# Two row-sum reciprocals in one VectorE instruction, in the first attention of a two-layer transformer kernel

## The chip, the core and the metric

The kernel runs on one core of one Trainium2 chip. The metric is the device time of one execution, in microseconds (us). An engine is TensorE (PE, with its weight loads shown as PEld), VectorE (DVE), ScalarE (ACT), GpSimd (POOL) or SyncE (SP, which here only issues DMAs). Each engine runs its own instructions strictly in the order in which they were written, and engines wait for each other on semaphores.

## The reference

Eight sequences of 1024 tokens with 256 features pass through two layers: attention, a block-quantised feed-forward, a second attention, and a mixture of low-rank experts. What the change touches is the first attention, cut to what matters:

```python
# x: (8, 1024, 256); 8 heads of 64; V = 32
q = (x @ Mq).reshape(B, H, C, K)          # a plain reshape: heads are mixed with rows
k = (x @ Mk).reshape(B, H, C, K)
v = (x @ Mv).reshape(B, H, C, V)
scores = jnp.einsum('bhqk,bhck->bhqc', q, k).reshape(B * H, C, C)
att = jax.nn.softmax(scores / jnp.sqrt(jnp.float32(K)), axis=1)   # over the queries
out = jnp.einsum('bqhc,bhcd->bqhd', att.reshape(B, C, H, C), v)
```

The softmax normalises over the queries, so each key has a maximum and a sum of its own. The kernel puts 128 keys on the partitions and all 1024 queries along the free dimension; the reciprocal of a key's sum can then be multiplied into that key's row of `v`, which is 32 wide, in place of its 1024 attention weights.

## The kernel before

The eight sequences (b = 0 to 7) are worked through in a software pipeline. One period holds, among others, the feed-forward and second attention of earlier sequences and, in its second part, the first attention of the next sequence (`attn0`) beside that sequence's remaining projections, the query/key preparation of the second attention and the expert layer of the one before. Every engine has its own lanes of generators; each `yield` gives a place in time, and `weave` merges the lanes of one engine by these places when the program is built. Nothing is reordered when it runs.

`attn0` has 64 steps for each sequence, one step for each block of 128 keys and one head. I write a step as (m), with m from 0 to 63; g = m // 8 and c = m % 8. A step goes through six stages on four engines:

- **S(m)**, PE, L459 into `pS`: 16 matmuls (four of 32 columns for each of two operand pairs and two halves) give 128 keys x 1024 queries. `pS` holds two steps, so S(m) waits for exponential (m-2), by semaphore `e0_in`.
- **R(m)**, DVE, L1239: the negated maximum of each row.
- **X(m)**, ACT, L914: the exponential, into one of four buffers `EA[m % 4]`, with the row sum accumulated into column c of `zz`, a tile of eight columns.
- **Z(m)**, DVE, L1256: the reciprocal of that column, into column c of `rz`. It stands at place m+1.45, behind R(m+1).
- **V(m)**, POOL, L1726: the slice of `v` times that reciprocal, into one of four buffers `vs[m % 4]`. It waits for `rz_in` to reach m+1.
- **P(m)**, PE, L560: eight matmuls (each seen as two records) of `vs` by `EA`, accumulated in `pV` over the eight steps of a group. It waits for `vs_in`. Its place is m+3.8, behind S(m+3) and ahead of S(m+4); for c = 0 it is m+4.1, behind S(m+4).

Between these, each engine's queue holds other lanes' work: on PE mostly projections (L459 into `pR`), on DVE the low halves of split operands (L1119), LayerNorm statistics (L1136, L1138), normalisations (L1142, L1272), sums of squares (L1545) and additions (L1133, L1233); on POOL a normalisation of the queries and keys of the second attention (L1814 to L1855). What L1855 writes goes to memory and back by SP's DMAs, and becomes the keys and queries of the second attention. A second attention and a feed-forward follow, whose input `xT` comes by a DMA transpose.

In `ffn_in` (L1272) and other lanes the numbers of steps that count on `pv0_in` or `o0_in` stay as they are. The three lanes of `attn0` on PE, ACT and POOL and the wait of V(m) on `rz_in` are not part of the diff.

Of the kernel before, what the change touches and what calls it, by code (L numbers as in the profile page):

```python
# [54 lines left out]
def build(nc, a, out):  # L55
    with ExitStack() as ctx:

        def sb(name, shape, dt=F32):
            return ctx.enter_context(nc.sbuf_tensor(name, shape, dt))

        def sem(name):
            return ctx.enter_context(nc.semaphore(name))
# [116 lines left out]
        zz = sb("zz", [128, 8])  # L179
        rz = sb("rz", [128, 8])  # L180
# [23 lines left out]
        s0_in, max0_in, e0_in, rz_in, vs_in, pv0_in = (sem(n) for n in ("s0", "max0", "e0", "rz", "vs", "pv0"))  # L204
# [42 lines left out]
        def bank(u):  # L247
            return pR[:, 512 * u.bank:512 * u.bank + 512]
# [858 lines left out]
        def _(e):  # L1107
            reg = e.alloc_register("flag_dve")

            def full(key):  # L1110
                u = ring[key]
                e.wait_ge(r_full[u.bank], u.n)
                return u
# [116 lines left out]
            def attn0(b):  # L1230
                def outputs(g):
                    u = full(("o0T", b, g))
                    e.tensor_tensor(x[b % 2][:, g, :], x[b % 2][:, g, :], bank(u)[:, 0:256], ALU.add).then_inc(r_free[u.bank], 1)  # L1233

                for n in range(69):
                    yield n
                    if n < 64:
                        e.wait_ge(s0_in, 64 * b + n + 1)
                        e.tensor_reduce(nmaxa[:, n % 32:n % 32 + 1], pS[:, 1024 * (n % 2):1024 * (n % 2) + 1024], AXX, ALU.max,  # L1239
                                        negate=True).then_inc(max0_in, 1)  # L1240
                    if n > 4 and (n - 5) % 8 == 7:
                        yield n + .35
                        outputs((n - 5) // 8)
                    if n > 3 and (n - 4) % 8 == 7:
                        yield n + .15
                        g = (n - 4) // 8
                        e.wait_ge(pv0_in, 64 * b + 8 * g + 8)
                        if g:
                            full(("o0T", b, g - 1))
                        e.tensor_copy(oTa[:, :], pV[:, 0:256]).then_inc(o0_in, 1)  # L1250
                    yield n + .45
                    if 0 < n < 65:
                        m = n - 1
                        c = m % 8
                        e.wait_ge(e0_in, 64 * b + m + 1)
                        e.reciprocal(rz[:, c:c + 1], zz[:, c:c + 1]).then_inc(rz_in, 1)  # L1256

            def ffn_in(b):
                xb = x[b % 2]
# [424 lines left out]
            def lanes_y(i):  # L1684
                return [*([first(i + 1, attn0), first(i + 1, projections)] if within(i + 1) else []),
                        *([placed(-6, prep()), placed(-6, prep_low()), prep_heads()] if i < 0 else []),
                        *([v for lane in (moe_x3, moe_gate, moe_M) for v in second(i - 1, lane)] if within(i - 1) else []),
                        *([heads(i), heads_bias(i), heads_norm(i)] if within(i) and i + 1 < NB else
                          [heads_end(), heads_bias(i), heads_norm_end(), heads_by_end(), heads_low_end()] if i + 1 == NB else [])]
# [562 lines left out]
```

## Time and profile before

| | us |
|---|---|
| median of 3 runs | 2958.23 |
| lowest and highest of these | 2956.24, 2965.4 |
| span of the profiled execution | 2954.7 |
| PE busy, share of the span | 2580.8, 87% |
| DVE busy | 2104.1, 71% |
| ACT busy | 1979.9, 67% |
| POOL busy | 1193.4, 40% |
| first attention of sequence 3, S(0) to the end of P(63) | 1031.08 to 1203.63 |

The span is the time between the first and last instruction in the profile, and the median of the unprofiled runs lies 3.5 us above it. The page's busy shares are means over all stages. The part to read is the second part of each period, in which `attn0` runs, and there the waits of one engine for another: views of the waits, the timeline of one engine, and the chain of work that ended last (followed back from the end, at each step to what released it).

### The profile page before, as it was taken

Reading aid. Unit: us, or ns where it says so; the run is one execution under the profiler, and the core shown is the slowest. Engines: PE = TensorE matmul, PEld = TensorE weight load, DVE = VectorE, ACT = ScalarE, POOL = GpSimd, SP = SyncE. Lnnn points to the kernel's source line nnn. Section 1 sums busy time; section 2 is a strip of 40 time slices with the busy share of each in tenths; the row PEclk is TensorE's granted clock in tenths of the full one; section 3 lists DMA queues with packets and bytes.
Section 4 is the critical chain, followed back from the end, with each engine's and each line's share of the span. In section 5 each row is a group of like instructions: output and inputs, shape, how many; then the busy total and the mean of one; then the engine's idle time right before and its main releaser. Section 6 shows DMA issues by size and latency. Waiting matters only on the chain.

```text
span 2954.7 us, 115301 instructions
## 1 busy us (share of the span) xinstructions
PE 2580.8 (87%) x50178; PEld 1403.9 (48%) x50178; DVE 2104.1 (71%) x4266; ACT 1979.9 (67%) x3763; POOL 1193.4 (40%) x1677
## 2 busy tenths in 40 slices
PE   4766786998989989999889989899889999899697
PEld 3434554445644466444554456444654446444233
DVE  6778766866778488875879578775788667775433
ACT  3541255876668866787668866787668776687684
POOL 3563156215642167223653156322662256411210
PEclk9997999999999999999999999999999999999798
DMA  4212332234424252323424253243423253222310
GB/s 127 44 38 46 67 84 69 50 49 86 97 64 81 47 111 62 77 51 73 109 63 75 34 108 79 58 78 58 103 70 66 49 86 84 63 67 47 87 31 16
DMA packets 470460, 203.52 MB, mean 69 GB/s; under 512 B 283289, under 2 KB 459937, under 8 KB 469929
## 3 DMA queue, kind: packets, MB, share of 16 engines
q1 hardware_dynamic: 467960, 194.07, 31.9%
q8 instruction: 413, 6.77, 0.9%
q10 hardware_dynamic: 1968, 1.72, 0.2%
q14 instruction: 119, 0.97, 0.1%
HBM read 46.48 MB, written 32.51 MB: 27 GB/s over the span
## 4 chain that ended last, share of the span: by engine, by line
PE 42%; DVE 29%; ACT 8%; SPq 7%; issue 7%; DMA 5%; POOL 2%; DVEq 0%; ACTq 0%; POOLq 0%
PE pR L459 18%; PE pV L690 9%; DVE nmaxa L1239 8%; PE pS L459 5%; PE pS L650 5%; ACT ub L953 5%; PE pV L560 3%; SPq L1958 2%; PE pR L469 2%; SPq L2155 2%; SPq L2141 1%; DMA xT<-ua 1%; DMA xT<-xhb 1%; DVE ua L1142 1%; DVE ua L1119 1%
## 5 line engine op out<-in xcount | busy, mean ns | idle before, releaser
L953 ACT ACTIVATE ub<-pS 128x512 f32<-128x512 f32 x2048 | 1048.2, 612 | 227.6 <-PE pS L650 227.0
L1239 DVE TENSOR_REDUCE nmaxa<-pS 128x1 f32<-128x1024 f32 x512 | 621.1, 1214 | 249.9 <-PE pS L459 247.2
L914 ACT ACTIVATE ua<-pS,nmaxa 128x1024 f32<-128x1024 f32 x384 | 427.9, 1114 | 406.1 <-DVE nmaxa L1239 403.9
L459 PE MATMUL pS<-ua 128*32 128x512 f16 x8192 | 544.1, 387 | 102.2 <-ACT ua L914 77.4
L690 PE MATMUL pV<-ub,vaug 128*17 128x512 f32 x4096 | 536.7, 597 | 14.6 <-DVE ub L1397 13.2
L1726 POOL TENSOR_TENSOR ua<-ua,rz 128x256 f32<-128x256 f32 x512 | 332.0, 650 | 429.4 <-DVE rz L1256 414.4
L650 PE MATMUL pS<-ub 50*128 50x512 f16 x1920 | 352.0, 386 | 27.6 <-DMA ub<-scr 11.6
L459 PEld LDWEIGHTS pS<-ua 128*32 128x32 f16 x8192 | 210.1, 98 | 273.9 <-ACT ua L914 110.4
L459 PE MATMUL pR<-wgu,xT 128*32 128x352 f16 x6144 | 284.9, 321 | 49.5 <-DMA xT<-ua 24.6
L650 PEld LDWEIGHTS pS<-ub 50*128 50x128 f16 x1920 | 96.5, 93 | 404.4 <-ACT ub L953 334.6
L560 PE MATMUL pV<-ua 128*32 128x128 f32 x6144 | 244.7, 279 | 22.6 <-DVE oTa L1250 12.2
L459 PEld LDWEIGHTS pR<-wgu,xT 128*32 128x32 f16 x6144 | 160.9, 99 | 188.1 <-issue 114.6
L914 ACT ACTIVATE EA<-pS,nmaxa 128x1024 f32<-128x1024 f32 x128 | 142.6, 1114 | 137.1 <-DVE nmaxa L1239 135.9
L560 PEld LDWEIGHTS pV<-ua 128*32 128x32 f32 x6144 | 169.3, 112 | 92.3 <-DVE oTa L1250 25.8
L459 PE MATMUL pR<-wqkv,xT 128*32 128x512 f16 (+1 forms) x3072 | 147.4, 330 | 13.8 <-DMA xT<-xhb 10.2
L1790 POOL CAST xhb<-at_ 128x256 f16<-128x256 f32 x56 | 24.1, 431 | 301.9 <-DVE at_ L1389 253.4
L1771 POOL TENSOR_TENSOR EA<-ua,EA 128x704 f16<-128x704 f32 x28 | 45.5, 1627 | 239.4 <-DVE EA L1348 239.4
L690 PEld LDWEIGHTS pV<-ub,vaug 128*17 128x17 f32 x4096 | 84.7, 96 | 114.4 <-issue 73.9
L459 PE MATMUL pR<-wd,ua 128*32 128x256 f16 x4032 | 130.5, 273 | 3.3 <-DVE ua L1307 1.9
L459 PEld LDWEIGHTS pR<-wd,ua 128*32 128x32 f16 x4032 | 103.9, 97 | 56.5 <-issue 47.9
L459 PE MATMUL pR<-xT,mq 128*32 128x256 f16 x3072 | 98.4, 279 | 26.2 <-DMA xT<-ua 25.2
L1297 DVE SCALAR_TENSOR_TENSOR ua<-ua,pR 128x352 f32<-128x352 f32 x112 | 57.5, 513 | 89.4 <-ACT ua L924 89.4
(262 smaller groups left out, 4062.6 us busy)
## 6 DMA issues: line engine op xcount, KB each, us to landing
ua<-ua SPq DMA_DIRECT2D x384, 128.0 KB, 2.7
ub<-scr SPq DMA_DIRECT2D x264, 64.0 KB, 2.9
scr<-ub SPq DMA_DIRECT2D x30, 512.0 KB, 3.8
x<-in_L_attn_x SPq DMA_DIRECT2D x8, 1024.0 KB, 6.2
between<-x SPq DMA_DIRECT2D x7, 1024.0 KB, 5.0
ub<-between SPq DMA_DIRECT2D x7, 1024.0 KB, 5.9
out<-ub SPq DMA_DIRECT2D x7, 1024.0 KB, 5.4
ub<-scr SPq DMA_DIRECT2D x192, 32.0 KB, 1.8
```

What stands on the lines that cost most here:

```text
L459: i = e.matmul(dst[j:j + 32], w[:, j:j + 32], m, start=start, stop=stop)
L469: return e.matmul(dst, src, ident[0:n, 0:n], is_transpose=True)
L560: i = e.matmul(pV[32 * jl:32 * jl + 32, 128 * jg:128 * jg + 128], vs[n % 4][:, j, :], EA[n % 4][:, 128 * j:128 * j + 128], start=(c == 0 a ...
L650: e.matmul(pS[:, 512 * hl:512 * hl + 512], kk_[row:row + 50, o, 128 * c:128 * c + 128], q[row:row + 50, o, 512 * qh:512 * qh + 512]).then_ ...
L690: i = e.matmul(pV[32 * hl:32 * hl + 17, :], vaug[:, c, 4 * hg + hl, :], EB[(4 * n + hl) % 8], start=(c == 0), stop=(c == 7))
L914: e.activation(EA[n % 4], pS[:, 1024 * (n % 2):1024 * (n % 2) + 1024], ACT.Exp, bias=nmaxa[:, n % 32:n % 32 + 1], accum_out=zz[:, n % 8:n ...
L953: e.activation(EB[(4 * n + hl) % 8], pS[:, 512 * hl:512 * hl + 512], ACT.Exp).then_inc(e1_in, 1)
L1239: e.tensor_reduce(nmaxa[:, n % 32:n % 32 + 1], pS[:, 1024 * (n % 2):1024 * (n % 2) + 1024], AXX, ALU.max, negate=True).then_inc(max0_in, 1)
L1297: e.scalar_tensor_tensor(ht[hv][:, FH:2 * FH], ht[hv][:, 0:FH], 1.0, bank(g)[:, 0:FH], ALU.add, ALU.mult).then_inc(r_free[g.bank], 1)
L1726: e.tensor_tensor(vs[m % 4], vv[:, :, 32 * c:32 * c + 32], rz[:, c:c + 1].unsqueeze(2).to_broadcast([128, 8, 32]), ALU.mult).then_inc(vs_i ...
L1958: e.dma_start(dst[r0:r0 + 64, par::2, o:o + 256], sh[64 * par:64 * par + 64, w, l, :, :]).then_inc(fill0[pair % 2], 16)
L2155: e.dma_start(dst[at:at + 16, o:o + 2, :], scr[b % 2, w_, l, 64 * hg:64 * hg + 64, :].rearrange("(h p d) n -> p d h n", p=2, d=16)[par]).t ...
```

## The change

In DVE's lane of `attn0`, even steps no longer have a reciprocal. At odd steps one instruction takes the reciprocals of two neighbouring columns, c-1 and c, and raises `rz_in` by two. The wait for `e0_in` at the odd step stands as before. The places in the order are unchanged, and so is every other lane.

```diff
                     if 0 < n < 65:
                         m = n - 1
                         c = m % 8
-                        e.wait_ge(e0_in, 64 * b + m + 1)
-                        e.reciprocal(rz[:, c:c + 1], zz[:, c:c + 1]).then_inc(rz_in, 1)
+                        if m % 2:
+                            e.wait_ge(e0_in, 64 * b + m + 1)
+                            e.reciprocal(rz[:, c - 1:c + 1], zz[:, c - 1:c + 1]).then_inc(rz_in, 2)
```

The order of DVE in the first attention of sequence 3, from R(44) to Z(47), before. Names are tiles, output first; `amx`, `small` and `ub` belong to other lanes, and the semaphores waited for stand in brackets:

```order
L1239 TENSOR_REDUCE nmaxa<-pS 128x1 [waits s0]
L1545 TENSOR_REDUCE small<-ub 128x64 [waits sq]
L1233 TENSOR_TENSOR x<-x,pR 128x256 [waits r_full0]
L1256 RECIPROCAL rz<-zz 128x1 [waits e0]
L1239 TENSOR_REDUCE nmaxa<-pS 128x1 [waits s0]
L1256 RECIPROCAL rz<-zz 128x1 [waits e0]
L1239 TENSOR_REDUCE nmaxa<-pS 128x1 [waits s0]
L1133 SCALAR_TENSOR_TENSOR ub<-pR,ub 128x256 [waits r_full1,xb2]
L1272 TENSOR_SCALAR ua<-x,agF,rstdF 128x256 [waits rstdF,fill0_1]
L1272 TENSOR_SCALAR ua<-x,agF,rstdF 128x256 x3
L1256 RECIPROCAL rz<-zz 128x1 [waits e0]
L1239 TENSOR_REDUCE nmaxa<-pS 128x1 [waits s0]
```

The same place in the changed kernel, whose later lines are numbered one higher:

```order
L1239 TENSOR_REDUCE nmaxa<-pS 128x1 [waits s0]
L1546 TENSOR_REDUCE small<-ub 128x64 [waits sq]
L1233 TENSOR_TENSOR x<-x,pR 128x256 [waits r_full0]
L1257 RECIPROCAL rz<-zz 128x2 [waits e0]
L1239 TENSOR_REDUCE nmaxa<-pS 128x1 [waits s0] x2
L1133 SCALAR_TENSOR_TENSOR ub<-pR,ub 128x256 [waits r_full1,xb2]
L1273 TENSOR_SCALAR ua<-x,agF,rstdF 128x256 [waits rstdF,fill0_1]
L1273 TENSOR_SCALAR ua<-x,agF,rstdF 128x256 x3
L1257 RECIPROCAL rz<-zz 128x2 [waits e0]
```

The reciprocal of step 44 between R(45) and R(46) is gone; step 44 is now served by the instruction behind the four L1272. The reciprocal ahead of R(45) serves steps 42 and 43. PE's order is the same in both kernels; its part of the same place, from P(42) to P(44), is this:

```order
L560 MATMUL pV<-ua 32x128 [waits vs]
L560 MATMUL pV<-ua 32x128 x7
L459 MATMUL pR<-wmoe,xT1 32x256 [waits r_free1]
L459 MATMUL pR<-wmoe,xT1 32x256 x23
L459 MATMUL pR<-bt,ub 32x256 [waits r_free2]
L459 MATMUL pR<-bt,ub 32x256 x11
L459 MATMUL pS<-ua 32x512 [waits e0]
L459 MATMUL pS<-ua 32x512 x15
L560 MATMUL pV<-EA3,ua 32x128 [waits vs]
L560 MATMUL pV<-EA3,ua 32x128 x7
L459 MATMUL pS<-ua 32x512 [waits e0]
L459 MATMUL pS<-ua 32x512 x15
```

Nothing has moved here: behind each P(m) stands the work that waits with it.

## Rows read from the trace of the kernel before

**Rows 1.** The page: busy us of each engine, share of the span, instructions.
```profile
PE 2580.8 (87%) x50178; PEld 1403.9 (48%) x50178; DVE 2104.1 (71%) x4266; ACT 1979.9 (67%) x3763; POOL 1193.4 (40%) x1677
```

**Rows 2.** Busy time by engine in sequence 3's first attention: window, length, PE, PEld, DVE, ACT, POOL.
```profile
1031.00:1204.00 173.00, 153.03 (x3818) 103.08 (x3822) 140.16 (x290) 109.09 (x195) 111.87 (x175) 0.99 0.40 91
```

**Rows 3.** The reciprocals, grouped by form: busy us, mean ns, idle before, releaser.
```profile
L1256 DVE RECIPROCAL rz<-zz 128x1 f32<-128x1 f32 x512 | 77.0, 150 | 10.4 <-ACT EA L914 9.6
```

**Rows 4.** Waits between 1031 and 1204 us: total us, times, longest.
```profile
POOL ua L1726 <- DVE rz L1256: 49.9, 31, 13.8
...
DVE nmaxa L1239 <- PE pS L459: 30.3, 21, 10.8
...
PEld pV L560 <- POOL ua L1726: 3.6, 8, 0.9
```

**Rows 5.** Timeline of DVE (start, length in us): Z(42), Z(43), Z(44), R(46), Z(45), L1153, Z(47).
```profile
1152.55 0.15 DVE L1256 RECIPROCAL rz<-zz 128x1 f32<-128x1 f32 x1
...
1156.06 0.15 DVE L1256 RECIPROCAL rz<-zz 128x1 f32<-128x1 f32 x1
...
1157.25 0.15 DVE L1256 RECIPROCAL rz<-zz 128x1 f32<-128x1 f32 x1
1157.32 1.21 DVE L1239 TENSOR_REDUCE nmaxa<-pS 128x1 f32<-128x1024 f32 x1
...
1160.52 0.15 DVE L1256 RECIPROCAL rz<-zz 128x1 f32<-128x1 f32 x1
...
1162.91 1.20 DVE L1153 TENSOR_REDUCE amx<-ua 128x64 f32<-128x1024 f32 x1
1164.03 0.15 DVE L1256 RECIPROCAL rz<-zz 128x1 f32<-128x1 f32 x1
```

**Rows 6.** Timeline of POOL: V(42) and V(50).
```profile
1152.85 0.61 POOL L1726 TENSOR_TENSOR ua<-ua,rz 128x256 f32<-128x256 f32 x1 [2.21 <-DVE rz L1256]
...
1173.03 0.61 POOL L1726 TENSOR_TENSOR ua<-ua,rz 128x256 f32<-128x256 f32 x1
```

**Rows 7.** Timeline of PE: P(42), S(46), S(47), P(44), P(46), P(50).
```profile
1154.53 0.62 PE L560 MATMUL pV<-ua 128*32 128x128 f32 x16
...
1155.98 1.05 PE L459 MATMUL pS<-ua 128*32 128x512 f16 x16
...
1158.63 1.05 PE L459 MATMUL pS<-ua 128*32 128x512 f16 x16 [0.96 <-ACT ua L914]
1159.81 0.64 PE L560 MATMUL pV<-ua 128*32 128x128 f32 x16
...
1163.96 0.61 PE L560 MATMUL pV<-ua 128*32 128x128 f32 x16
...
1173.69 0.65 PE L560 MATMUL pV<-ua 128*32 128x128 f32 x16 [0.44 <-POOL ua L1726]
```

**Rows 8.** The chain that ended last, 1170 to 1198 us, in order of time.
```profile
1171.13 1.95 POOL ub L1855
...
1192.68 4.37 DMA xT<-ua
```

**Rows 9.** Timeline at step 2 of sequence 3: P(2), S(6), Z(3), S(7).
```profile
1044.20 0.61 PE L560 MATMUL pV<-ua 128*32 128x128 f32 x16
...
1045.21 1.05 PE L459 MATMUL pS<-ua 128*32 128x512 f16 x16 [0.40 <-ACT ua L914]
...
1045.57 0.13 DVE L1256 RECIPROCAL rz<-zz 128x1 f32<-128x1 f32 x1
...
1048.71 1.05 PE L459 MATMUL pS<-ua 128*32 128x512 f16 x16 [0.49 <-ACT ua L914]
```

**Rows 10.** Timeline in sequence 1: P(6), the projection behind it, Z(7).
```profile
350.12 0.61 PE L560 MATMUL pV<-ua 128*32 128x128 f32 x16
...
353.21 1.60 PE L459 MATMUL pR<-wgu,xT 128*32 128x352 f16 x24 [2.48 <-DVE ua L1119]
...
353.50 0.15 DVE L1256 RECIPROCAL rz<-zz 128x1 f32<-128x1 f32 x1
```

## The prediction

> **What bounds the kernel now.** I read the page first [rows 1]. PE is busy for 87% of the span and DVE for 71%, so neither is at its limit over the whole. The change only touches the first attention, which runs in about 172 us of each period of some 338 us, so I went to that stretch for sequence 3 [rows 2]. There PE is busy for 153 of 173 us and DVE for 140, while ACT and POOL have 60 us or more to spare. It is a stage of two nearly full engines in fixed order, each waiting now and then for the other.
>
> The waits of the stretch come next [rows 4]. POOL waits for reciprocals for 49.9 us, which is harmless where POOL has nothing late behind it. PE waits for POOL's product V(m) for only 3.6 us (its weight loads, 8 times). DVE waits 30.3 us for scores. The reader should see that V(m) is waited for little because it is early, on average over the even steps about 2.7 us before PE wants it, and that this margin is what the change spends.
>
> **What is removed.** Of 512 reciprocals 256 go [rows 3]. One shows 150 ns, but the next DVE instruction starts 0.07 us behind its start (1157.25 and 1157.32) [rows 5]. So DVE gets back between 256 x 0.07 = 18 us and 256 x 0.15 = 38 us over the whole kernel. I take 0.07, because that is the pitch in the queue. Widening the rest from 128x1 to 128x2 I put at nothing; the 128x256 product on POOL shows no trace of a form that small, and the bound is the whole 0.07 us on the 256 that stay, which would cancel the gain. The gain counts only where DVE sets the pace. In sequence 3 the chain of work that ended last, read step by step up to step 50, passes through about ten of the reciprocals that go, so I count 10 x 0.07 = 0.7 us there, or at most all 32 x 0.07 = 2.2 us.
>
> The Trainium skill (VectorE: DVE Perf Modes, section on the TRN2 errata) says that VectorE pays a fixed cost for each instruction and asks for fewer, larger ones. By its 58 cycles plus one per element at 0.96 GHz the second column costs 1 ns and an instruction saved gives back 61 ns, 16 us in all. The row of 0.07 us agrees. The rule speaks for the change; it says nothing on who waits for the result.
>
> The wait for the exponentials at odd steps is the old one, and reciprocals hardly waited before (10.4 us in 512) [rows 3]. So DVE gets no new wait ahead of other work.
>
> **What is added.** Z for an even step m is now Z(m+1), behind R(m+2) in DVE's queue, so V(m) starts later by one step, on average 2.5 us. The queued work behind V(m) on POOL (the normalisation of queries and keys, L1831 to L1855) waits with it, and V(m+1) comes behind both, where V(m) and that work used to be done before Z(m+1). Behind P(m) on PE wait the projections and S(m+4), and for that wait R(m+4), X(m+4) and so on.
>
> The earliest P(m) is Z(m+1) + 0.30 (from Z(42) to V(42)) + 0.61 (V's length) + 0.05 (V(50) starts at 1173.03 and lasts 0.61; P(50), which waited for it, starts at 1173.69) [rows 5 to 7]. That is Z(m+1) + 0.96. Comparing this with the start of P(m) for all 32 even steps of sequence 3, 13 are late, by 14.1 us together. The first is step 2: 1045.57 + 0.96 - 1044.20 = 2.33 us [rows 9]; the largest is step 42: 1156.06 + 0.96 - 1154.53 = 2.49 us [rows 5, 7]. Sequences 2 and 4 to 7 give 14.0 to 14.6 each, sequence 0 17.5 and sequence 1 21.8 (there step 6 is late by 353.50 + 0.96 - 350.12 = 4.34 us) [rows 10]. All eight: 125 us. This is the first-order stall if nothing absorbs it.
>
> **What absorbs it, worked at two places.** Steps 42 to 50 first. P(42) goes from 1154.53 to 1157.02. S(46) follows from 1155.98 to 1158.47, ends at 1159.52, and R(46) starts at 1159.57 where it started at 1157.32: 2.25 us late, DVE being idle meanwhile. Z(45) comes 3.20 us behind R(46) as before, so at 1162.77, and V(44) needs it now: P(44) at 1163.73 against 1159.81, 3.92 late. S(47) lies between and had waited 0.96 us for an exponential; that wait vanishes and PE waits at P(44) instead. S(48) ends some 1.5 us behind P(44) (0.45 for P's pitch, an estimate from its length of 0.64, and 1.05), R(48) follows, and L1153 moves from 1162.91 to about 1166.4, Z(47) from 1164.03 to 1167.5. P(46) is then at 1168.5 against 1163.96, 4.5 late [rows 5, 7]. DVE had some 0.4 us of slack at R(50), so 4.1 us pass on to step 50. First-order, these three steps were late by 2.49 + 1.67 + 1.03 = 5.2; four fifths pass.
>
> After step 50 the chain leaves PE. It runs from POOL's L1855 at 1171.13 over a store and SP's issues to the transpose at 1192.68, for which PE then waits [rows 8]. Step 50 and later (1.04 + 0.35 + 0.70 + 0.07 us) are hidden beside that.
>
> At step 2, S(6) had waited 0.40 us and follows P(2) after 0.45, so it moves by 2.33 less the 0.56 between them, 1.8 us. S(7) had waited another 0.49 us, with a little more behind P(3); about 1.1 us reaches R(7) [rows 9]. Steps 10, 12 and 14 (3.0 us together) are late on PE while DVE sets the pace, with over 1 us of slack between S and R: nothing passes. Step 34 (0.82) passes 0.4.
>
> **The sum.** For sequence 3: 1.1 + 0.4 + 4.1 - 0.7 = 4.9 us. That is 0.35 of its 14.1. Six sequences like it: 29 us. For sequences 0 and 1 I take the same share, 0.35 x 39.3 = 14 us; in sequence 1, step 6 supports it, as PE had idled 2.48 us behind P(6) and 4.34 shrinks to some 1.7. In all 43 us. The profiled span of 2954.7 would become 2998, and the median lies 3.5 above the span: 2958.2 + 43 = 3001 us.
>
> **Rivals.**
>
> *Everything passes.* A delayed step also delays the DVE work from which the next pair's reciprocal follows, as between 42 and 44, where 1.67 became 3.92. The loop Z(m+1), V, P(m), S(m+4), R(m+4), Z(m+3) now closes over two steps (5.4 us at 2.7 a step) and itself takes 0.96 + 0.45 + 1.05 + 1.2 plus what stands between on PE and DVE; before, it had three. If this loop sets the pace in most of the stage, four fifths or all of 125 us pass: 3058 to 3083. Against it speak steps 10 to 14. Chance 0.12.
>
> *DVE's relief wins: faster.* Place: DVE's queue in the second part of each period. It decides if the stalls at P fall almost wholly into waits PE has anyway (the 2.48 at step 6 of sequence 1, the 0.96 at S(47)), and then 18 us at most come back, 38 if the whole record counts: 2940, at the very best 2920. It needs less than 0.1 of the 125 us to pass. By the skill's per-instruction rule named above the time would be 2942. Steps 42 to 46 speak against it, each of the six times. Chance 0.06.
>
> *Nothing to be seen.* Stalls of 10 to 20 us and a relief of the same size: 2950 to 2967. Chance 0.09.
>
> *It doesn't do what it says.* The even columns might be read before they are ready; but the wait at m covers m-1 as ACT works in order, so no time hangs on it.
>
> **How the numbers follow.** The forecast, 20 to 75 us slower, has 0.73. The range reaches from 2968 (a quarter of the step 42 effect, or sequences 0 and 1 giving nothing and DVE's relief counted whole) to 3062 (four fifths of 125 us), leaving about 0.2 out. A measurement of this kernel tells 0.3% (9 us) from no change. Faster 0.06, same 0.09, slower 0.85.
>
> **What the profile after would show.** Right: L1257 with 256 instructions of about 150 ns in the form 128x2; PE's wait for L1726 in a steady sequence's stretch up from 3.6 us to 10 or more, mostly ahead of even P(m); DVE's wait for scores up from 30.3 us; the first attention of sequence 3 longer by about 5 us, the rest of the period unchanged. P(42) and P(44) should have waits, P(43) none. Wrong: if PE's waits for POOL grow and its waits for exponentials shrink by as much, the stalls were absorbed, and the relief shows. If the stage grows by 12 us or more, the loop over two steps rules. If 128x2 reciprocals show far over 150 ns, the relief is gone as well.

## The result, and the profile after

| | before | after |
|---|---|---|
| median, us | 2961.07 (4 runs) | 3023.02 (4 runs, 3016.98 to 3023.76) |
| ratio after / before | | 1.0214, 95% interval 1.0194 to 1.0234 |
| span of the profiled execution, us | 2954.7 | 3015.1 |
| first attention of sequence 3, us | 172.55 | 180.34 |

The change makes the kernel 2.1% slower, 62 us. The sign, the main mechanism and the range of the prediction hold; its size, 43 us, was too small, and one term that it had put at nothing was not. Measured from S(0) to the end of P(63), the eight first attentions are longer by 14.0, 5.3, 5.7, 7.8, 10.9, 2.7, 5.6 and 7.5 us, 59.5 us together; the whole rest of the program is 0.9 us longer. So the time is lost where the edit is. How it spreads over the sequences is less certain, as this is one profiled execution against one: the six steady stages (sequences 2 to 7) of the kernel before, whose order of work is alike, lie between 171.4 and 176.0 us.

The page of the kernel after, its busy times and the groups of P and V (columns as in [rows 1, 3]):

```profile
PE 2592.2 (86%) x50178; PEld 1420.4 (47%) x50178; DVE 2087.2 (69%) x4010; ACT 1980.6 (66%) x3763; POOL 1181.8 (39%) x1677
...
L1727 POOL TENSOR_TENSOR ua<-ua,rz 128x256 f32<-128x256 f32 x512 | 319.7, 631 | 585.3 <-DVE rz L1257 567.1
...
L560 PE MATMUL pV<-ua 128*32 128x128 f32 x6144 | 247.6, 281 | 146.4 <-POOL ua L1727 133.4
```

VectorE has 256 instructions and 16.9 us of busy time less, near the 18 us of the pitch of 0.07 us and far from the 38 us of the records. It is no exact measure of them: two kernels further down that leave out the same number of reciprocals show 12.0 and 22.0 us less, as the durations of other VectorE instructions move too. The reciprocals by form:

```profile
L1257 DVE RECIPROCAL rz<-zz 128x2 f32<-128x2 f32 x256 | 39.3, 154 | 11.3 <-ACT EA L914 10.7 <-issue 0.2 <-ACT ua L914 0.2
```

An instruction shows 154 ns for two columns against 150 for one [rows 3], and the idle time in front of them is the same 10 or 11 us in all. The instruction itself is as cheap as hoped. What it does to others stands in the waits of sequence 3's first attention, 1054.8 to 1235.3 us, to be held against [rows 4]:

```profile
POOL ua L1727 <- DVE rz L1257: 69.2, 26, 15.6
...
DVE nmaxa L1239 <- PE pS L459: 39.4, 28, 10.8
PEld pV L560 <- POOL ua L1727: 26.2, 20, 3.0
PE pV L560 <- POOL ua L1727: 17.3, 16, 2.5
```

TensorE's weight loads for P waited for V 8 times and 3.6 us; now it is 20 times and 26.2 us. VectorE waits 9 us more for scores, and the 32 reciprocals that are gone in this stage gave it back only 2.2 us (32 x 0.07). The timeline of PE at the worked example, P(42), S(46), S(47), P(44) and P(46), against [rows 7]:

```profile
1183.79 0.64 PE L560 MATMUL pV<-ua 128*32 128x128 f32 x16 [2.25 <-POOL ua L1727]
...
1185.23 1.05 PE L459 MATMUL pS<-ua 128*32 128x512 f16 x16
...
1186.53 1.05 PE L459 MATMUL pS<-ua 128*32 128x512 f16 x16
1190.05 0.64 PE L560 MATMUL pV<-ua 128*32 128x128 f32 x16 [2.47 <-POOL ua L1727]
...
1194.85 0.64 PE L560 MATMUL pV<-ua 128*32 128x128 f32 x16 [1.02 <-POOL ua L1727]
```

And DVE at Z(43), R(46), Z(45), R(48), L1153 and Z(47), against [rows 5]:

```profile
1182.82 0.16 DVE L1257 RECIPROCAL rz<-zz 128x2 f32<-128x2 f32 x1
...
1186.32 1.23 DVE L1239 TENSOR_REDUCE nmaxa<-pS 128x1 f32<-128x1024 f32 x1 [2.23 <-PE pS L459]
...
1189.08 0.15 DVE L1257 RECIPROCAL rz<-zz 128x2 f32<-128x2 f32 x1
...
1191.60 1.22 DVE L1239 TENSOR_REDUCE nmaxa<-pS 128x1 f32<-128x1024 f32 x1 [1.24 <-PE pS L459]
1192.74 1.21 DVE L1153 TENSOR_REDUCE amx<-ua 128x64 f32<-128x1024 f32 x1
1193.86 0.15 DVE L1257 RECIPROCAL rz<-zz 128x2 f32<-128x2 f32 x1
```

The reader should see the whole chain in these eleven lines. Z(43) starts at 1182.82 and P(42) at 1183.79, 0.97 us later (0.96 was forecast). S(46) comes 1.44 us behind P(42) as before (1.45), R(46) has to wait 2.23 us for it, Z(45) comes 2.76 us behind R(46), and P(44) 0.97 behind that. Taken against the stage's own start, this place is 3.0 us late at R(42) and 6.7 at R(50): 3.7 us were added (4.1 forecast). The wait of 0.96 us that S(47) had for an exponential is gone, as said.

### The profile page after: what moved, and what is told of

Read it like the earlier page. It is cut to its first block, busy times and chain, and to the rows that moved or that the text cites. A ratio compares the mean times of both kernels' runs of the same rounds, so it can differ in the third digit from the quotient of the medians.

```text
span 3015.1 us, 115301 instructions
## 1 busy us (share of the span) xinstructions
PE 2592.2 (86%) x50178; PEld 1420.4 (47%) x50178; DVE 2087.2 (69%) x4010; ACT 1980.6 (66%) x3763; POOL 1181.8 (39%) x1677
## 4 chain that ended last, share of the span: by engine, by line
PE 43%; DVE 26%; issue 8%; ACT 7%; SPq 6%; POOL 5%; DMA 5%; DVEq 0%; POOLq 0%; ACTq 0%
PE pR L459 18%; PE pV L690 8%; PE pS L459 6%; DVE nmaxa L1239 5%; PE pS L650 5%; ACT ub L953 5%; PE pV L560 4%; PE pR L469 2%; SPq L1959 2%; POOL ua L1727 2%; SPq L2156 2%; DMA xT<-xhb 1%; DMA xT<-ua 1%; DVE ua L1142 1%; SPq L2142 1%
## 5 line engine op out<-in xcount | busy, mean ns | idle before, releaser
L1727 POOL TENSOR_TENSOR ua<-ua,rz 128x256 f32<-128x256 f32 x512 | 319.7, 631 | 585.3 <-DVE rz L1257 567.1
L459 PEld LDWEIGHTS pS<-ua 128*32 128x32 f16 x8192 | 226.8, 99 | 180.2 <-ACT ua L914 37.0
L560 PEld LDWEIGHTS pV<-ua 128*32 128x32 f32 x6144 | 162.6, 111 | 239.3 <-POOL ua L1727 189.8
L469 PE MATMUL pR<-ident,ub 128*128 128x128 f32 x522 | 85.6, 292 | 43.1 <-POOL ub L1920 16.5
```

Source lines behind the costliest of these rows:

```text
L459: i = e.matmul(dst[j:j + 32], w[:, j:j + 32], m, start=start, stop=stop)
L469: return e.matmul(dst, src, ident[0:n, 0:n], is_transpose=True)
L560: i = e.matmul(pV[32 * jl:32 * jl + 32, 128 * jg:128 * jg + 128], vs[n % 4][:, j, :], EA[n % 4][:, 128 * j:128 * j + 128], start=(c == 0 a ...
L1727: e.tensor_tensor(vs[m % 4], vv[:, :, 32 * c:32 * c + 32], rz[:, c:c + 1].unsqueeze(2).to_broadcast([128, 8, 32]), ALU.mult).then_inc(vs_i ...
```

## The experiments

Four theories stood against each other. **A**: TensorE stalls at P of even steps, since V has lost its margin, and a part passes on. **B**: GpSimd's other work, queued behind a V that waits, is what is late. **C**: removing or widening reciprocals has a cost of its own. And for the size: at which steps and sequences the loss arises. Each ratio is against the kernel before on the same chip; the medians of before were 2957.9 to 2960.4 us. "Gaps" ahead of P or S are the idle time of PE just before them, summed over the steps named; stages are measured from S(0) to the end of P(63).

### Delay without relief

```diff
-                    e.wait_ge(rz_in, 64 * b + m + 1)
+                    e.wait_ge(rz_in, 64 * b + m + (1 if m % 2 else 2))
```

> The kernel before with all its 512 reciprocals; only V(m) of an even step waits for the reciprocal of step m+1 as well. It makes the delay of the change without its relief on VectorE. Theory A (TensorE stalls at P of even steps, a part passes on, relief worth 0 to 18 us): 3023 to 3041 us, +62 to +80 against before, with TensorE's waits for L1726 at about 14 us a steady sequence. Theory B (GpSimd's queue behind V is what is late): the same time, as its queue waits the same. Theory C (removing or widening reciprocals itself costs something): clearly below 3023, 3000 or less.

Measured: 3031.74 us, ratio 1.0247 (1.0227 to 1.0266). With all 512 reciprocals in place, one wait on GpSimd costs what the change costs and some 10 us more (the two intervals overlap by a little). In sequence 3 TensorE waits for V just as in the changed kernel:

```profile
PEld pV L560 <- POOL ua L1726: 26.2, 21, 3.0
PE pV L560 <- POOL ua L1726: 17.1, 15, 2.5
```

So the delay alone makes the whole loss, and C is out. A and B are not told apart by this run.

### Relief without delay

```diff
-                        e.wait_ge(e0_in, 64 * b + m + 1)
-                        e.reciprocal(rz[:, c:c + 1], zz[:, c:c + 1]).then_inc(rz_in, 1)
+                        if m % 2:
+                            e.wait_ge(e0_in, 64 * b + m + 1)
+                            e.reciprocal(rz[:, c:c + 1], zz[:, c:c + 1]).then_inc(rz_in, 1)
...
-                    e.wait_ge(rz_in, 64 * b + m + 1)
+                    if m % 2:
+                        e.wait_ge(rz_in, 32 * b + m // 2 + 1)
+                    else:
+                        e.wait_ge(e0_in, 64 * b + m + 1)
```

> Relief without delay. The reciprocals of even steps are left out and V(m) of an even step multiplies by a constant 1 (so even steps are not normalised); it waits for the exponential of its own step instead. 256 reciprocals stay, 128x1. Theory A: 2943 to 2961 us, a gain of 0 to 18 us (256 x 0.07) and TensorE's small waits for V gone. Theory C: no gain, or a loss of more than 5 us.

The line of V itself, which takes the constant at even steps, is left out of the diff.

Measured: 2956.91 us, ratio 0.999 (0.9977 to 1.0002), a gain of 3 us that can't be told from none. The 12.0 us by which VectorE is less busy in this profile buy next to nothing: in sequence 3 it waits 32.1 us for scores, where it had waited 30.3 [rows 4].

```profile
DVE nmaxa L1239 <- PE pS L459: 32.1, 23, 10.7
```

What was saved in its queue is mostly waited for a little later.

### P later, under the pairing

```diff
-                    if 3 < n < 68 and n % 8 == 4:
+                    if 3 < n < 68 and n % 2 == 0:
                         yield n + .1
                         values0(b, n - 4)
...
-                    if 2 < n < 67 and n % 8 != 3:
+                    if 2 < n < 67 and n % 2 == 0:
                         values0(b, n - 3)
```

> The changed kernel, with P of even steps moved from behind S(m+3) to behind S(m+4), where P of c = 0 stood already. Nothing else moves. Theory A: the margin of P grows by about one S and what stands beside it, the stalls at P shrink to a third or less, and at least two thirds of the 62 us come back: 2980 us or less. Theory B (GpSimd's queue is late and with it the keys and queries of the second attention): GpSimd waits as long as in the changed kernel, 3005 us or more.

Measured: 2987.13 us, ratio 1.0094 (1.0075 to 1.0112). Of 62 us 35 came back, between the two thresholds: more than B allows and less than A asks. The gaps ahead of even P fell from 14.6 to 1.7 us in sequence 3, as A said, but some 27 us stayed. In the profiled execution, the slowest of four, the stages are 36.9 us longer than before: 11.5 in sequence 0, 7.4 in sequence 1 and 18.0 in the six steady ones together. In sequence 0's stretch, 47 to 243 us, this stands among the waits:

```profile
PE pR L469 <- POOL ub L1920: 20.6, 11, 4.5
```

In the kernel before it was 7.5 us there, in the changed kernel 15.2. L1920 is GpSimd's last step of quantising the feed-forward weights, which TensorE then transposes; it has nothing to do with the attention but stands in the same queue as V. That is B.

In the steady sequences B reaches TensorE by another way, V of the odd steps. V(m+1) stands behind the work that waited with V(m), and P(m+1) is late with it. The gaps ahead of odd P are 0.0 us in sequence 3 before, 2.8 in the changed kernel and 5.9 here, for instance at P(15):

```profile
1101.41 0.65 PE L560 MATMUL pV<-EA,ua 128*32 128x128 f32 x16 [1.33 <-POOL ua L1727]
```

So a part of the stall at P is itself GpSimd's queue.

### V later in GpSimd's order, under the pairing

```diff
-                    yield m + 1.8
+                    yield m + 1.8 if m % 2 else m + 2.75
```

> The changed kernel, with V(m) of even steps put straight ahead of V(m+1) in GpSimd's order (place m+2.75 for m+1.8), so that GpSimd's other work no longer queues behind a V that waits. V itself is as early as its reciprocal allows. Theory A: within 10 us of the changed kernel, 3013 to 3033. Theory B: at least half of the 62 us come back, 2992 or less.

Measured: 3018.6 us, ratio 1.0201 (1.0183 to 1.022). By itself this gives 4 us against the changed kernel, and the two intervals overlap, so it may be nothing. The gaps at even P in sequence 3 are 15.0 us, as they were (14.6). GpSimd's queue is cleared all the same. TensorE's wait for L1920 in sequence 0, 47 to 245 us:

```profile
PE pR L469 <- POOL ub L1920: 2.5, 2, 2.1
```

It was 15.2 us, and the gaps ahead of odd P fell from 20 to 0.4 us over the eight stages. Yet sequence 0's stage is 198.0 us long where it was 198.7: with TensorE stalled at even P, clearing the queue shortened almost nothing there. Had I stopped here, B would have been given up.

### Both moves, and the control

The two edits above together, under the pairing:

> The changed kernel with both moves: P of even steps behind S(m+4) and V of even steps straight ahead of V(m+1) on GpSimd. With P's move alone 28 us stayed, 11 of them in sequence 0, where TensorE waits for GpSimd's quantised weights (L1920) for 20.6 us against 7.5 before. If what stays there is GpSimd's other work queued behind a waiting V, this move takes it away: 2978 us or less, and the wait for L1920 under 12 us. If not: 2982 or more.

Measured: 2960.76 us, ratio 1.0006 (0.9992 to 1.0019). All 62 us are gone, within 6 us. The gaps ahead of odd P are 0.8 us over the eight stages. TensorE's wait for L1920 in sequence 0, 47 to 237 us:

```profile
PE pR L469 <- POOL ub L1920: 5.3, 5, 2.5
```

The control has P's move in the kernel before, with all reciprocals:

> Control for the kernel with P of even steps moved behind S(m+4): the same move in the kernel before, with all 512 reciprocals. If the move itself costs (P later holds a buffer of exponentials longer), this is 10 us or more above before, and the 28 us that were left in the changed kernel with this move are partly that. If not, it is within 9 us of before.

Measured: 2956.06 us, ratio 1.0002 (0.9989 to 1.0014). P's move alone is worth nothing without the pairing, so the 35 us that it gave back are the pairing's own cost. V's move has no such control. There were two paths side by side: TensorE's stall at even P, and GpSimd's queue behind V. Clearing GpSimd's alone gives 4 us or nothing, TensorE's alone 35, both 62. While TensorE stalls at even P, GpSimd's lateness is largely covered.

### Where the loss arises

Here the pairing is made in some places and the rest is as before; `place` stands for `b == 0`, or for b > 1 and the steps named.

```diff
+                        if place:
+                            if m % 2:
+                                e.wait_ge(e0_in, 64 * b + m + 1)
+                                e.reciprocal(rz[:, c - 1:c + 1], zz[:, c - 1:c + 1]).then_inc(rz_in, 2)
+                        else:
+                            e.wait_ge(e0_in, 64 * b + m + 1)
+                            e.reciprocal(rz[:, c:c + 1], zz[:, c:c + 1]).then_inc(rz_in, 1)
```

> The pairing in sequence 0 alone. The profile after had this stage 14.0 us longer. If the cost is local to the stage, +10 to +16 us against before; if the sequences' costs only show in the sum (or come from elsewhere), +6 or less.

> The pairing only at steps 42/43, 44/45 and 46/47 of sequences 2 to 7 (18 pairs of 256). The worked example of the prediction gives 4.1 us a sequence, less 0.2 of relief: 6 x 3.9 = +23 us. Rival: the loss builds up over the whole stage and three pairs alone are absorbed: +10 us or less.

> The pairing only at steps 10/11, 12/13 and 14/15 of sequences 2 to 7. The prediction said that nothing passes there: 0 us, within 3. The profile after has step 17's scores and maxima about 2 us later than steps 8 and 9 in sequence 3, so by it each sequence loses 1.7 to 2.1 us: +10 to +13 us.

> The pairing at steps 0 to 21 of sequences 2 to 7. The prediction has 1.1 us a sequence (from step 2), less relief: +6 us. The profile after has sequence 3 3.25 us late at step 20: +19 us. If this run exceeds the one with steps 10 to 15 by about 6 us, step 2 was sized right and the miss is steps 10 to 14.

> The pairing only at steps 50 to 63 of sequences 2 to 7. The prediction counts these as hidden beside GpSimd's last product for the second attention and the transfers behind it: 0 us, within 4. Rival: they pass like the others, first-order 2.2 us a sequence at four fifths: +10 us.

| pairing only at | ratio (95% interval) | us | prediction, us |
|---|---|---|---|
| sequence 0 | 1.0034 (1.0016 to 1.0051) | +10 | +6 |
| 42 to 47, sequences 2 to 7 | 1.0081 (1.005 to 1.0112) | +24 | +23 |
| 10 to 15, sequences 2 to 7 | 1.0035 (1.002 to 1.005) | +10 | 0 |
| 0 to 21, sequences 2 to 7 | 1.0068 (1.0047 to 1.0089) | +20 | +6 |
| 50 to 63, sequences 2 to 7 | 1.0013 (0.9995 to 1.003) | +4 | 0 |

The microseconds are the ratio's excess times 2960; the interval of 42 to 47 reaches from 15 to 33 us, and the medians there differ by 30. Sequence 0, steps 0 to 21, 42 to 47 and 50 to 63 add to 58 us, and sequence 1's stage is 5.3 us longer in the profile after: 63 against 62 measured. The intervals of the four together leave some 13 us either way, so an agreement this close is in part luck. Steps 22 to 41, 48 and 49 of the steady sequences had no run; in the profile after, sequence 3 is 3.2 us late at S(22) and 3.0 at S(42), so nothing was added between. As far as this can tell, the pieces are local and add up.

Three pairs of 32 in each steady sequence, 42 to 47, whose first-order lateness is the largest (5.2 us of 14.1), make 24 of the 62 us. The run at steps 10 to 15 was the one that went against the prediction, and its profile says why. Sequence 3, POOL's timeline at V(10) and V(12), then GpSimd's last low half for the expert layer's input, then the chain that ended last in the same stretch (start us, length us, what):

```profile
1072.40 0.92 POOL L1731 TENSOR_TENSOR ua<-ua,rz 128x256 f32<-128x256 f32 x1 [2.64 <-DVE rz L1258]
...
1077.01 0.61 POOL L1731 TENSOR_TENSOR ua<-ua,rz 128x256 f32<-128x256 f32 x1 [1.50 <-DVE rz L1258]
...
1085.51 1.16 POOL L1803 TENSOR_TENSOR xhb<-ub,xhb 128x512 f16<-128x512 f32 x1
```
```profile
1078.31 1.17 POOL xhb L1803
...
1083.17 1.12 POOL xhb L1803
...
1086.75 5.15 DMA xT<-xhb
...
1092.25 0.44 PE pR L469 x2
```

PE's timeline there (L469 is a pair of small transposes whose bank ACT's L964 frees, and L964 waited for that DMA):

```profile
1092.25 0.44 PE L469 MATMUL pR<-ident,oTa 128*128 128x128 f32 x2 [2.40 <-ACT xhb L964]
```

GpSimd waits 2.64 us at V(10) and 1.50 at V(12), where it waited 0 and 0.84 before. Its low halves of the expert layer's input (L1803, L1798 in the kernel before) come later: against the stage's own start the last of the four ends 1.1 us later than before. The transposing DMA is issued 0.08 us behind that end, lands 5.15 us after its issue where it took 4.54 before, and TensorE waits 2.40 us at L469. The chain view names a projection on TensorE just ahead of the DMA; the issue stands right behind L1803. The longer transfer, 0.6 us of it, isn't shown to come from the edit: the same transfer takes between 4.2 and 6.2 us from one sequence to the next before. In the steps between, S(14) is 1.2 us late and R(14) 0.1, so the slack between scores and maxima takes the stall up as the prediction said, and some of S and R of steps 15 to 20 come up to 1.0 us early. At step 21 everything is 1.6 us late. The path to that was not scores and maxima; it was GpSimd's queue.

### A version for the steady sequences

Pairing and both moves in sequences 2 to 7 only, 0 and 1 as before:

> An attempt at a version that beats both: pairing, P of even steps behind S(m+4) and V of even steps ahead of V(m+1), all only in sequences 2 to 7; sequences 0 and 1 as before. With the moves in all sequences the time was that of before, with sequence 0 5.0 and sequence 1 2.7 us longer and the steady ones 0.6 us shorter each. So 2950 to 2956 us if that is real, 2958 if the relief is worth nothing.

Measured: 2955.1 us, ratio 0.9986 (0.997 to 1.0002). It may be a gain of 4 us; the interval does not exclude none, and I don't call it faster.

## Why the prediction was right, and where it was short

**What bounds the kernel**: right. Two nearly full engines in fixed order, and a margin ahead of P. All of the loss arose in the stage named.

**Relief**: about right in its size in the queue (18 us forecast; 16.9 us less busy time, 12.0 and 22.0 in the two other kernels that leave out 256) and about right in its worth. I had given it 0.7 us in a steady sequence, 4 over six; leaving the reciprocals out without delay gave 3 in all, and the pairing compared with the pure delay 10, each with several us of noise.

**The price of the delay**: Z(m+1) + 0.96 was met (0.97 at P(42) and P(44)). The first-order stall of 125 us is seen too: gaps ahead of even P rose from 22 to 136 us over the eight stages. PE's gaps ahead of S fell from 102 to 37, which is the absorption the forecast spoke of. Gaps ahead of odd P, for which the forecast had nothing, rose from 2 to 20.

**Steps 42 to 50**: right, 23 us forecast and 24 measured for six sequences, with an interval from 15 to 33.

**Steps 2 to 8**: 1.1 us a sequence; the pairing at 0 to 21 less that at 10 to 15 gives 10 us, 1.6 a sequence, with intervals of some 4 to 6 us either way on each, and steps 16 to 21 are in it too. In sequence 3 of the profile after, R(7) is 1.1 us late, as worked out.

**Steps 10 to 14, "nothing passes"**: this step failed. It measured 1.7 us a sequence (1.0 to 2.5). I compared P with the slack between S and R, all on the PE and DVE side, and there the reading was right. The prediction had named GpSimd's queue behind V and never priced it; at this place it feeds a transpose that TensorE waits for.

**Sequence 0**: mis-sized. I carried the steady share of 0.35 over to it (6 us); it measured 10 us (5 to 15), 14 in the profile. The experiments with the two moves point to the same omission: the weights' quantisation stands in GpSimd's queue. Sequence 1 was taken 2 us too high against one profile (7.6 and 5.3), which is within its noise.

**Step 34** passed nothing in the profile (0.4 a sequence forecast). **Steps 50 and later**: 0 forecast, 4 us measured with an interval from -1 to 9; left open. In sequence 3 of the profile after, the maxima are 6.7 us late at step 50, 10.5 at step 60, and the stage ends 7.8 late, so most of what arose there was taken up again by the end, as the forecast had it.

**The range**: its upper end, 3062, was to be four fifths of 125 us, which give 3058. Nothing hangs on it.

**The rivals.** That everything passes is out: 62 of 125 us. The place 42 to 46 comes near it (3.7 us added of 5.2), the rest doesn't; sequence 3's stage grew by 7.8 us, between the 5 forecast and the 12 that were to show a loop over two steps. VectorE's relief winning is out by the run with relief alone, which has no delay at all and gains 3 us. The Trainium skill's charge for each instruction (VectorE: DVE Perf Modes, section on the TRN2 errata), by the estimate above 16 us for 256 instructions, agrees with VectorE's busy time here, 12.0 to 22.0 us less; it is no measure of the kernel's time.

## What to carry to other kernels

Before two small instructions are joined at the later one's place, list for each consumer how long before its use the first result was ready, and compare that with the delay; here 32 such differences for each sequence gave the first-order stall within a tenth (125 us against 114), though not how much of it would pass. Then follow both queues that the delayed result stands in, that of its user and that of the engine between: over the whole program the second was largely covered by the first and showed when the first was cleared, or at steps 10 to 15, where it set the time by itself. A cheap instruction on an engine that waits a little later anyway is worth almost nothing.

## What the hardware showed that I had not expected

The four 128x256 normalisations of VectorE at the worked place (L1272 before, L1273 after) took 1.83 us before and 1.37 after. The first line is the kernel before, the second the kernel after:

```profile
1158.77 1.83 DVE L1272 TENSOR_SCALAR ua<-x,agF,rstdF 128x256 f32<-128x256 f32 x4
```
```profile
1187.79 1.37 DVE L1273 TENSOR_SCALAR ua<-x,agF,rstdF 128x256 f32<-128x256 f32 x4
```

GpSimd worked beside them before. After, it stood idle from 1187.93 to 1189.38, waiting for the reciprocal behind these very four. So a part of the delay paid itself back, 0.46 us here. The 64 such instructions of each kernel point the same way: with no GpSimd instruction beside them, 25 before and 46 after took 398 to 410 ns each; the 16 before that had it beside them for nine tenths or more of their time took 411 to 1131 ns, 636 on average. That GpSimd's work slows VectorE is my reading of this; no run varied it alone.
